# First attention: VectorE takes the outputs' low part behind the unit's maximum in place of ahead of the difference

## What is computed

```python
s1 = q1 @ k1 * scale ; s2 = q2 @ k2 * scale     # two score maps of each of 16 heads, masked to a window of 64
a1 = softmax(s1) ; a2 = softmax(s2)
diff = relu(a1 - lam * a2)
diff = diff / (sum(diff) + 1e-06)
out = diff @ v                                  # 128 tokens x 128 of each head
x = x + concat(out) @ Wo
```

## Time and profile before

| | |
|---|---|
| median of 3 runs | 1347.83 us (1346.96 to 1347.96) |
| span of the profiled execution, first to last instruction | 1343.3 us |
| PE busy | 1269.2 us, 94% |
| DVE busy | 843.1 us, 63% |
| ACT busy | 715.6 us, 53% |
| POOL busy | 470.9 us, 35% |

### The profile page before, as it was taken

How to read it: one execution, slowest core, us unless ns; L and a number is a source line. 1 busy time by engine, 2 the same in 40 slices (tenths; PEclk the granted TensorE clock), 3 DMA queues, 4 the chain that set the end, 5 groups by cost and what they waited for, 6 DMA issues and landing times.

```text
span 1343.3 us, 27486 instructions
## 1 busy us (share of the span) xinstructions
PE 1269.2 (94%) x9712; PEld 989.2 (74%) x9712; DVE 843.1 (63%) x1986; ACT 715.6 (53%) x2746; POOL 470.9 (35%) x467
## 2 busy tenths in 40 slices
PE   5799999999999788999999999989899999999998
PEld 4578888888887565666666666557788888888887
DVE  6788888888888676666656656765453333433333
ACT  2788888889887553444444444465232332423322
POOL 3122113112212134544544534541053353533532
PEclk9999999999999899999999999999999999999999
DMA  6011001100102101002002001000325342254230
GB/s 221 16 25 49 18 17 25 49 17 17 31 19 92 35 1 76 1 1 76 1 1 75 1 1 60 1 1 1 107 58 142 74 120 56 39 137 78 56 93 31
DMA packets 29810, 64.54 MB, mean 48 GB/s; under 512 B 6912, under 2 KB 12160, under 8 KB 28416
## 3 DMA queue, kind: packets, MB, share of 16 engines
q1 hardware_dynamic: 29696, 63.05, 17.6%
HBM read 52.42 MB, written 2.23 MB: 41 GB/s over the span
## 4 chain that ended last, share of the span: by engine, by line
PE 74%; DVE 10%; ACT 7%; issue 4%; POOL 2%; DMA 2%; SPq 1%; DVEq 0%; POOLq 0%; ACTq 0%
PE ps L531 31%; PE ps L923 9%; PE ps L647 5%; PE ps L716 4%; PE ps L679 4%; PE ps L820 4%; ACT ea L1434 3%; PE ps L810 3%; PE ps L792 3%; PE ps L800 2%; PE ps L670 2%; PE ps L586 2%; DMA cw<-comb_d 2%; ACT ea L1478 1%; DVE xnt L991 1%
## 5 line engine op out<-in xcount | busy, mean ns | idle before, releaser
L1798 POOL TENSOR_TENSOR sg<-sg,cw 128x512 f32<-128x512 f32 x88 | 113.5, 1290 | 260.1 <-ACT sg L1597 253.1
L1375 DVE TENSOR_TENSOR hh<-ps,sg 128x512 f32<-128x512 f32 x100 | 69.2, 692 | 178.6 <-POOL sg L1798 162.0
L1401 ACT ACTIVATE hhh<-hh 128x512 fp32r<-128x512 f32 x100 | 63.2, 632 | 214.7 <-DVE hh L1375 214.7
L1401 ACT ACTIVATE pt<-ps 128x512 f32<-128x512 f32 x128 | 76.9, 600 | 179.3 <-PE ps L800 122.6
L1434 ACT ACTIVATE ea<-ps,negmax 128x64 f32<-128x64 f32 (+1 forms) x512 | 164.6, 341 | 6.0 <-DVE negmax L1127 6.0
L531 PE MATMUL ps<-xnh,wch 128*128 128x512 f32 x400 | 157.0, 393 | 0.7 <-ACT pt L1401 0.7
L1174 DVE TENSOR_TENSOR qcs<-ps,tabb 128x512 f32<-128x512 f32 x192 | 123.6, 686 | 53.4 <-PE ps L531 53.1
L531 PE MATMUL ps<-xnl,wch 128*128 128x512 f32 x400 | 156.9, 392 | 0.0
L531 PE MATMUL ps<-xnh,wcl 128*128 128x512 f32 x400 | 155.6, 389 | 0.0
L1665 POOL TENSOR_TENSOR ea<-ea,rden 128x128 f32<-128x128 f32 (+1 forms) x128 | 62.1, 506 | 256.2 <-DVE rden L1083 256.2
L1672 POOL TENSOR_TENSOR eb<-eb,rsum 128x512 f32<-128x512 f32 x64 | 66.9, 1045 | 160.3 <-DVE rsum L1218 160.3
(11 more groups left out here) (153 smaller groups left out, 3349.6 us busy)
## 6 DMA issues: line engine op xcount, KB each, us to landing
raw_w<-in_rawb_dram SPq DMA_DIRECT2D x4, 2432.0 KB, 9.0
kva<-ktmp SPq DMA_DIRECT2D x64, 128.0 KB, 2.4
cw<-comb_d SPq DMA_DIRECT2D x32, 256.0 KB, 5.0
raw_w<-in_rawc_dram SPq DMA_DIRECT2D x4, 1920.0 KB, 8.0
cw<-comb_d SPq DMA_DIRECT2D x16, 224.0 KB, 4.3
raw_a<-in_wqk_dram SPq DMA_DIRECT2D x4, 768.0 KB, 5.4
cw<-comb_d SPq DMA_DIRECT2D x16, 192.0 KB, 6.0
cw<-comb_d SPq DMA_DIRECT2D x16, 160.0 KB, 5.5
```

What stands on the lines that cost most here:

```text
L1375: dve.tensor_tensor(hh[:, par, :], bank(C_U[par]), sg[:, par, :], ALU.mult).then_inc(c_h, 1)
L1401: return act.activation(dst, src, ACT.Copy)
L1798: pool.tensor_tensor(sg[:, par, :], sg[:, par, :], cw[:, c % 2, t, :], ALU.mult).then_inc(c_hs, 1)
```

## The change

The low part's block, with its two waits, is moved from ahead of the difference to behind the maximum. Nothing is added or removed, and no other engine's program changes.

```diff
                 if one:
                     a_rho(n - 1, (u - 1) % 2, g if u else g - 1)
-                if not (first and u < 3) and not (drain and u >= 3):
-
-                    dve.wait_ge(a_o, n - 2)
-                    wait(dve, a_wo, n - 4)
-                    dve.tensor_tensor(by_head(oal[:, (u - 3) % 2, :, :]), by_block(bank(OB)),
-                                      by_head(oah[:, (u - 3) % 2, :, :]).bitcast(f32), ALU.subtract).then_inc(a_ol, 1)
                 if one:
                     a_diff(n - 1, (u - 1) % 2)
                 if not drain:
...
                     dve.tensor_reduce(most[:, :, XP:HG], late(A_S[u % 2]), axis=AX.X, op=ALU.max, negate=True)\
                        .then_inc(a_mx, 1)
+                if not (first and u < 3) and not (drain and u >= 3):
+
+                    dve.wait_ge(a_o, n - 2)
+                    wait(dve, a_wo, n - 4)
+                    dve.tensor_tensor(by_head(oal[:, (u - 3) % 2, :, :]), by_block(bank(OB)),
+                                      by_head(oah[:, (u - 3) % 2, :, :]).bitcast(f32), ALU.subtract).then_inc(a_ol, 1)
                 if u == 3 and not drain:
```

## The result

| | before | changed |
|---|---|---|
| median of the runs | 1347.39 us (4 runs, 1345.82 to 1347.96) | 1366.08 us (4 runs, 1365.84 to 1368.23) |
| span of the profiled execution | 1343.3 us | 1364.0 us |
| ratio of times | | 1.0143, 95% interval 1.0128 to 1.0157 |

The change makes the kernel 1.4% slower: 18.7 us by the medians, 20.7 us by the two profiled executions. The forecast was 1370 us, in a range of 1359 to 1382.

A forecast was written before the change was run, and what follows sets the result against it. PE was taken to bound the even stretch (2.16 us idle of 300.62). Chunks 20.6 + GpSimd's hold 2.4 + wol 2.0 - credits 1.0 and 1.5 = 22.5 us on span 1343.3, so 1365.8; with 4.5 around it 1370, range 1359 to 1382.

The forecast's parts named there:

- The place of the loss: PE stops ahead of PV, waiting for the low part, in j = 0, 1 and 2; with j = 3 loss 0, at most 0.1.
- The size of a chunk: Losses of 0.49, 0.67, 0.31 and 0 for j = 0 to 3: 1.47 us a chunk, 20.6 us over 14 chunks.
- The recovery in j = 2: Earlier relu and later PE let rec start at S + 0.53 (S: scores' start), cutting the loss from 0.79 or more to 0.31.
- no recovery: Rival: exponentials come no earlier, or each wait costs PE the full weight load; 2.56 us a chunk, 1385 us; chance 0.10.
- GpSimd's hold, u = 10: In three units u = 10, POOL's L1653 holds rho, making the low part later: 0.8 us more each, 2.4 us in all.
- wol, u = 3: In four units u = 3, the low part pushes back wol, which Y waits for: 0.5 us each, 2.0 us.
- The credits: Two gains: PE's existing waits for DVE's slot(1) work, -1.0 us, and the DVE-relu-exponentials chain at the attention's end, -1.5 us.
- Waits of before: Part of PE's 2.16 us idle is waits for DVE's slot(1) work, which a later PE avoids: -1.0 us (0 to -2.2).
- The signs: From 99 us: PE idle some 22 us, named at PV's load; PV later in j = 0 to 2; clock 1.00; nothing moves behind 520.
- The clock: Rival: PE's stops bring its granted clock down to the lower level; up to +70 us, 1430 us; chance 0.03.
- Half the loss: Rival: the pipeline settles so that DVE runs ahead; 0.3 + 0.6 us a chunk, 12.6 us, 1362 us in all; chance 0.12.
- Faster: Rival: low part released by S + 3.34 (S: scores' start) everywhere, PV never late, only credits left; 1345 us; chance 0.05.

The follow-up runs named there:

- the released kernel: Against the changed kernel: low part made from the high part alone, PV waits only for the high part, Y still for the low part; 1351.13 us, ratio 1.0033.
- the stops of single places: Against the kernel before: low part behind the maximum only in units with j = 1 (1355.42 us), or only with j = 0 (1349.37 us).

## Why the prediction was right

**The place of the loss.** Right. PE's stops stand at PV, under the low part's name, in j = 0, 1 and 2 and not in 3. Taking PV's wait away brings the units back to within 1.0 us of before.

**The size of a chunk.** Forecast 1.47 us, measured 1.83. PV's own delays were 0.53, 0.83, 0.38 and 0.04 against 0.49, 0.67, 0.31 and 0. Two terms were mis-sized. The step from the low part's end to PV was taken as 0.05 plus 0.05 for the load, and 0.15 was measured. The 0.05 came from a matmul of Y in the drain, and Y's first matmul in the released kernel shows it again (210.34 to 210.39); PV's is longer. And the difference starts 0.61 behind rec where 0.49 was taken from the low part's old place, and in j = 1 at S + 1.50 for 1.39: the low part did not wait for rho's result, the difference does, so the low part had been filling that wait. From one S to the next each stop in j = 1, 2 and 3 costs some 0.08 more than PV's delay; PV's two passes last 1.10 us in the timeline when nothing runs ahead of them, in place of 1.02.

**The recovery in j = 2.** The size was right, half of the reason was not. rec came at S + 0.45 where 0.53 was forecast, but with the relu held back it still came at S + 0.61, for 1.06 before: PE's own lateness does most of it, the earlier relu the rest. The rival "no recovery" (1385) fell by this as well.

**GpSimd's hold, u = 10.** Forecast 0.8 us each beyond j = 2's loss, measured 4.24 - 3.72 = 0.52 in PV's delay. The whole unit went from 7.83 to 8.48 us, 0.65 more for 0.46 in an ordinary j = 2: it had waited before. It is ratio now that is held, 220.35 + 0.68 = 221.03, until POOL's L1653 ends at 219.59 + 1.42 = 221.01:

```profile
219.59 1.42 POOL L1653 TENSOR_TENSOR wal<-raw_a,wah 128x256 fp32r<-128x256 f32 x2
219.70 1.56 PE L647 MATMUL ps<-kva,qab 128*64 128x128 f32 x32
220.35 0.68 DVE L1062 TENSOR_TENSOR ratio<-rec,sums 128x4 f32<-128x4 f32 x1
223.94 0.67 PE L670 MATMUL ps<-pt,kva 128*128 128x512 f32 x1 [0.74 <-DVE oal L1127]
```

The rule of the Trainium skill (SBUF — State Buffer, "Who interferes with whom") agrees again, to 0.02 us: VectorE with two SBUF inputs waits for a GpSimd instruction that reads SBUF and started first.

**wol, u = 3.** Forecast 2.0 us for four, measured 6.04 - 5.82 = 0.22 each, 0.9. Against before even this is not a loss: the three of these units behind unit 4 took 6.01, 6.17 and 5.99 us before, with a projection that started late (the first waited 0.27 for ACT's `kva`), and 6.04 now. Y's first load does wait 0.78 for it, but most of this is in PV's shadow, as the released kernel shows for the low part.

**The credits.** Waits of before: forecast 1.0 us, read off PE's idle time. They were larger, because part of them doesn't show there as idle. PV is 0.53 late in j = 0, and yet the step to the next scores grows by 0.34. From Y's last matmul to those scores it took 1.86 us before (176.90 to 178.76), with a wait for the keys' product, and takes 1.60 now (183.32 to 184.92), without. With that inside, 13.5 chunks at 1.83, three holds at 0.52 and the three wols behind unit 4 at 0.22 make 26.9 us, against 22.5 measured in the units; so another 4.4 us of old waits were absorbed. They stood in the units that took longer before: u = 3 and u = 10 as above, u = 12 (7.68 us before, 7.72 now, for 7.38 and 7.72 in an ordinary j = 0), and unit 57, which lost 0.13 in place of 0.91. At the end 1.5 was forecast and 1.1 measured, and 0.6 came at the start, ahead of unit 4.

**The sum.** 22.5 us forecast on the span, 20.7 measured: losses of 25.0 for 26.9 measured, credits of 2.5 for 4.4 + 1.1 + 0.6 = 6.1. It came out closer than its parts, since losses and credits were both too small; that closeness is luck, the place of the loss and its order of size are not. The 4.5 us that I put around the span is wrong too: the changed kernel's profiled execution took 1365.86 us with a span of 1364.0, so 1.9 lie around it, and by the same 1.9 the profiled run of before took some 1345.2 (an estimate), less than its median.

**The signs.** PV behind the scores came as named (3.8, 4.0, 3.6 and 3.3 forecast; 3.87, 4.18, 3.72 and 3.37 measured), the clock stayed 1.00, the relu no longer waits for the difference, and behind 520 us nothing moved. Three didn't hold. PE's idle time rose to 15.6 us and not to some 22. The wait for the low part is named at PV's matmul, while its load says "issue". And "a unit with j = 0 takes 6.2 us in place of 5.70" was misread: 5.70 is the step that starts at j = 1 or 3, with nothing in slot(0); the step from j = 0 took 7.38 and takes 7.72. The sum did not use it.

**The rivals.** The clock kept 1.00 through the stops, so that one fell. "Half the loss" fell with the stops of single places, which were not made good. "Faster" fell with PV at S + 3.7 to 4.2.

## What to carry to other kernels

Before moving an instruction later on an engine with slack, find the first instruction elsewhere that waits for it, measure its room from a fixed point of the loop, and compare it with the durations that it is moved behind. Half of this move (0.92 of 1.84 us) fitted into the room and cost at most 0.2%, the other half made up the rest of the 1.4%. An instruction can free two things, and here the one that decided was not the reader of its result but the next writer of the buffer that it reads. And a bound engine's small waits, even where its busy share is 99%, can swallow a part of a loss that is put on it.

## What the runs showed that I had not expected

A stopped PV costs more than the low part's lateness: it starts 0.15 us behind VectorE's end, and the step to the next scores grows by some 0.08 us more than its delay. That this is the lost overlap with the passes ahead is my reading, of the modelled 1.10 us for 1.02. Idle time on PE's row is a modelled figure: it rose by 13.5 us in a stretch of 300, in which the units fell behind by some 18.

In the transition PV took 2.05 us for its two passes at 481.13 us, for 1.10 elsewhere, with a granted clock of 0.72 between 478 and 490 us; before, the clock in the answering stretch of 457 to 470 us was 0.81. The clock fell in the transition of both kernels and not in the even stretch. The fall of before at 452 us, behind a wait of PE of 2.61 us, is missing in the changed kernel; its own began between 479 and 480 us (0.78, then 0.50), behind a wait of 2.68 us that ended at 478.29.

```profile
478.00:490.00 12.00, 9.49 (x87) 7.29 (x88) 8.70 (x29) 5.89 (x29) 2.21 (x4) 0.72 0.00 1
```
